# Three edits to the issue order of a fused four-layer kernel: the first two weighings of a block made adjacent, the start of the second block rearranged, and the value copies of the second block moved ahead of its exponentials

## The reference, cut to what matters

```
x = x + pooled_attention(x)          # tanh scorer, masked softmax over 32 tokens, weighted sum of tokens
x = x + multi_head_attention(x)      # 16 heads of 8, softmax(Q K^T * scale + bias) V, then Wo
x = x + low_rank_expert_ffn(x)       # relu(x Wi + common + expert[row]) Wo + common + expert[row]
x = x + gelu_ffn(x)                  # gelu(x fc1 + b), 96 shared columns + 32 columns of expert[row]
```

## Time and profile before

| | us |
|---|---|
| median of 3 runs | 261.66 (261.25 to 266.24) |
| the profiled execution, whole time | 262.47 |
| its span from first to last instruction | 260.7 |
| PE busy | 248.1 (95% of the span) |
| DVE busy | 186.5 (72%) |
| ACT busy | 137.7 (53%) |
| POOL busy | 120.2 (46%) |

### The profile page before, as it was taken

How to read it: one execution, slowest core, us unless ns; L and a number is a source line. 1 busy time by engine, 2 the same in 40 slices (tenths; PEclk the granted TensorE clock), 3 DMA queues, 4 the chain that set the end, 5 groups by cost and what they waited for, 6 DMA issues and landing times.

```text
span 260.7 us, 12683 instructions
## 1 busy us (share of the span) xinstructions
PE 248.1 (95%) x4866; PEld 184.0 (71%) x4866; DVE 186.5 (72%) x349; ACT 137.7 (53%) x253; POOL 120.2 (46%) x242
## 2 busy tenths in 40 slices
PE   7899999888999999999999999999999999988994
PEld 5575556666687867787777768686878587857983
DVE  4879877874878877888878787878787878562031
ACT  3075563374628745673748382757196437542250
POOL 5867513454516452554445443536154436455330
PEclk9999999999999999999999999999999999999999
DMA  6979304640355216530554045603554541165011
GB/s 184 381 236 266 83 3 162 237 173 5 100 212 204 100 24 238 204 140 0 211 208 184 0 164 204 236 0 121 201 203 177 215 174 43 57 230 205 3 43 43
DMA packets 27326, 38.27 MB, mean 147 GB/s; under 512 B 10769, under 2 KB 11537, under 8 KB 27170
## 3 DMA queue, kind: packets, MB, share of 16 engines
q1 hardware_dynamic: 26578, 36.99, 39.7%
q10 hardware_dynamic: 720, 0.89, 1.3%
HBM read 10.60 MB, written 2.10 MB: 49 GB/s over the span
## 4 chain that ended last, share of the span: by engine, by line
PE 84%; DVE 8%; ACT 3%; issue 2%; DMA 2%; POOL 0%; ACTq 0%; DVEq 0%; POOLq 0%
PE pB L783 12%; PE pB L866 9%; PE pB L736 7%; PE pB L740 6%; PE pooled L711 6%; PE pB L737 6%; PE pooled L679 5%; PE pV L726 4%; PE pV L691 3%; PE pooled L673 3%; PE pV L732 2%; PE pooled L640 2%; PE pB L818 2%; DMA cols_s<-cols_dram 2%; PE pB L843 1%
## 5 line engine op out<-in xcount | busy, mean ns | idle before, releaser
L403 POOL COPY rw<-e3t_s 128x128 f32 x128 | 38.6, 302 | 55.1 <-issue 51.2
L382 POOL TENSOR_TENSOR sc<-sc,rmax 128x512 f32<-128x512 f32 x32 | 33.6, 1051 | 49.8 <-DVE rmax L1164 49.8
L783 PE MATMUL pB<-rwo,hid 128*32 128x128 f32 x1024 | 33.6, 275 | 1.2 <-issue 1.2
L507 ACT ACTIVATE ex<-sc 128x512 f32<-128x512 f32 x32 | 20.2, 630 | 27.2 <-POOL sc L382 26.7
L783 PEld LDWEIGHTS pB<-rwo,hid 128*32 128x32 f32 x1024 | 26.6, 109 | 5.1 <-issue 4.0
L1159 DVE SCALAR_TENSOR_TENSOR sc<-pooled,bias 128x512 f32<-128x512 f32 x32 | 21.7, 678 | 11.3 <-PE pooled L711 9.7
L413 POOL COPY rwo<-weff 128x512 f32 x32 | 21.9, 688 | 14.2 <-issue 5.6
L1170 DVE STREAM_TRANSPOSE pt<-ex 128x512 f32<-128x512 f32 x32 | 22.4, 701 | 7.2 <-ACT ex L507 7.1
L511 ACT ACTIVATE hid<-pB 128x512 f32<-128x512 f32 x32 | 18.3, 595 | 14.8 <-PE pB L740 14.6
L866 PE MATMUL pB<-rw,hT 128*32 128x128 f32 x768 | 24.4, 274 | 0.0
L1164 DVE TENSOR_REDUCE rmax<-sc 128x16 f32<-128x512 f32 x32 | 22.0, 686 | 1.1
(11 more groups left out here) (181 smaller groups left out, 521.7 us busy)
## 6 DMA issues: line engine op xcount, KB each, us to landing
rwo<-weff SPq DMA_DIRECT2D x96, 256.0 KB, 2.3
rw<-fc2t_dram SPq DMA_DIRECT2D x4, 768.0 KB, 12.3
xT<-xt_dram SPq DMA_DIRECT2D x7, 256.0 KB, 2.6
xN<-xn_dram SPq DMA_DIRECT2D x7, 256.0 KB, 2.9
out_dram<-o_s SPq DMA_DIRECT2D x7, 256.0 KB, 2.3
e3t_s<-e3t_dram SPq DMA_DIRECT2D x1, 1024.0 KB, 10.6
rwo<-ffn_w_dram SPq DMA_DIRECT2D x1, 896.0 KB, 6.3
rwo<-ffn_w_dram SPq DMA_DIRECT2D x1, 512.0 KB, 11.3
```

The lines of the kernel that those rows point to most:

```text
L382: pool.tensor_tensor(sc[:, g % 2, :, :], sc[:, g % 2, :, :], rmax[:, g % 2, :].unsqueeze(2).to_broadcast([P, H, S]), ALU.subtract).then_in ...
L403: pool.tensor_copy(rw[:, r, :, SHARED:D], e3t_s[:, bass.ds(e, 1), :, :].rearrange("p o c n -> p (o c) n"))\
L783: last = mm(pB2[S * q:S * q + S, P * g:P * g + P], hid[:, c, tok], rwo[:, Q4 * g + q, c, :], start=(c == 0), stop=(c == FC - 1))
```

## The change

It has three parts, and all of them are changes of order.

- In every `step_of(n)` for n from 1 to 7, PE issues `weigh(n, 0)` behind chunk 2 of the hidden layer in place of ahead of it, so that it stands directly in front of `weigh(n, 1)`.
- In front of step 1, PE issues `attn_out(0)` and `pooling(1)` ahead of `pairs_out(1)`, and `keep_busy(4, ...)` there is dropped. The waits are fitted to that: `pooling(1)` waits for `weff_sb` 2, `low(0)` for `weff_sb` 5, and the wait for all eight copies stands behind `low(0)`. ACT does `x2_high(0)` first and the four copies of the second half behind it, in the order 2, 0, 1, 3, and each of them waits for all products of `pairs_out(1)` (`weff_ps` 8).
- In step 1 alone, ACT does `values(1)` ahead of `l0_exps(2)` and `exps(1, 0)`, in place of behind them.

```
@@ ACT @@
             def expert_out(half, j):
-                act.wait_ge(weff_ps, Q4 * half + j + 1)
+                act.wait_ge(weff_ps, 2 * Q4 if half == 1 else j + 1)
...
             weight_highs(N_I, W_I, F)
+            x2_high(0)
+            expert_out(1, 2)
             expert_out(1, 0)
             expert_out(1, 1)
-            expert_out(1, 2)
             expert_out(1, 3)
-            x2_high(0)
...
                     token_major(last)
+                if last is None:
+                    values(n)
                 if next_block:
                     l0_exps(n + 1)
                 exps(n, 0)
-                values(n)
+                if last is not None:
+                    values(n)
                 exps(n, 1)
@@ PE @@
             base_out(1, 3)
+            attn_out(0)
+            pe.wait_ge(weff_sb, 2)
+            pooling(1)
             pairs_out(1)
-            pe.wait_ge(w_high, 2)
-            attn_out(0)
-            pe.wait_ge(weff_sb, 5)
-            pooling(1)
-            pe.wait_ge(weff_sb, 6)
-            keep_busy(4, pS0, ffn_p[0])
...
                 if last is None:
-                    pe.wait_ge(weff_sb, 2 * Q4)
+                    pe.wait_ge(weff_sb, Q4 + 1)
+                    pe.wait_ge(w_high, 2)
                     pe.wait_ge(w_low, 1)
                     low(n - 1)
+                    pe.wait_ge(weff_sb, 2 * Q4)
...
                 hidden_expert(n - 1, 1)
-                weigh(n, 0)
                 hidden(n - 1, 2)
                 hidden_expert(n - 1, 2)
+                weigh(n, 0)
                 weigh(n, 1)
```

## The result

| | before | changed |
|---|---|---|
| median of 5 runs, us | 261.66 | 258.51 |
| profiled execution, us | 262.47 | 258.46 |
| its span, us | 260.7 | 256.7 |

The ratio of the changed kernel's time to the time before is 0.9894, with a 95% interval of 0.9874 to 0.9914: 1.1% faster, within the 2% named in the prediction. Some executions took about 4 us longer, two of the five before among them (266.2 and 266.3; without them its median is 261.42): the ratios leave such runs out, and two later profiles that fell on one, at a granted clock of 0.98, are not read. The forecast was 258.6. The number was met; the way to it, as the rest of this text shows, was different in each of the three parts.

A forecast was written before the change was run, and what follows sets the result against it. PE, busy for 95% of the span, was taken as the bound. 0.93 + 1.0 + 1.4 = 3.3 us gave 259.1 from the profiled execution or 258.3 from the median; 258.6 was taken, range 257.2 to 260.8.

The forecast's parts named there:

- The front: Start of step 1: without the four idle-filling products the queries start at 39.46 against 40.39, gaining 0.93 us if nothing is late.
- the 0.21 put on the filler alone: Start of step 1: deleting only the idle-filling products, without the swap, would gain 0.21 us, as queries wait for `x1T`.
- The values: Step 1: block 1's value copies move into ACT's idle time, removing PE's whole 1.0 us wait; bounds 0.6 to 1.0.
- The pair: First two weighings in a row: one turn of 0.2 us less in each of 7 steps, 1.4; bounds 0 to 2.5.
- The gathers: Last `out_rows` group of step 1: PE arrives at 58.57, last gather lands about 58.6; a tie counted as 0.
- rival 1: Gathers hold PE up in step 1: first gather slips 2.0 us, PE waits 1.4, time 260.0; chance 0.14.
- first sign of being wrong: In the changed profile, PE waiting for the gathers of the last group would show the prediction wrong.
- The stall of 1.18: PE's "issue" gap in step 1's last output group, likeliest instruction fetch, left as it is; bounds 0 and 2.1 us.
- rival 3: The instruction-fetch stall in step 1 goes or is covered, saving 1.2 us more: 257.4; chance 0.07.
- The base: The 3.3 us sum gives 259.1 from the profiled 262.47, or 258.3 from the runs' median 261.66; 258.6 taken.
- Rivals 2: The pair of weighings brings nothing while the other two parts hold: 260.0; chance 0.13.
- rival 4: Loop body no longer stays resident: five passes each pay a 1.18 us fetch stall, 5.9 in all, 264.5; chance 0.04.

## Why the prediction was right, and where it wasn't

The time came out as forecast, 258.51 for 258.6, and the sign and size stand. The parts do not: that the sum held is luck, errors of nearly the same size on either side.

1. **The front, 0.93.** The queries' and DVE's times came as worked out (keys on DVE at 41.36, forecast 41.41; 0.95 at `values(1)`). The step that failed is "if nothing is late next": the copies into `weff` end 2 later, POOL's copies with them, and they lie on DVE's `lowp_l`, 0.98 for 0.69. That makes 0.65 at the scores. The time gave 0.65 alone, and nothing measurable beside the pair. That `x1T` needs the pairs as cover was right (0.78 of wait without them); the 0.21 put on the filler alone was 0.
2. **The values, 1.0.** Right alone (1.06). Wrong in the sum: the prediction priced each part against the kernel before. The pair moves the first weighing by 1.4, behind the end of the copies, and by itself covers the same wait. Beside it the edit is worth at most the 0.54 that PE would wait for the transposition, and the times don't show even that. The prediction had both numbers, the copies' end at 52.98 and chunk 2 ahead of the weighing, and didn't set them side by side.
3. **The pair, 1.4.** Undersized. Per step 0.2 of turn was right (one product at 0.43 fewer), and two weighings take 0.70 in place of 0.80, which makes 0.3. What the sum lacked is the last step, 0.96 where 0.2 was counted, since POOL's and DVE's instructions no longer meet there, and step 1, 0.71 where 0.2 was counted, with the covered wait in it. Measured alone: 3.1 us by the medians and the profiles, above the upper bound of 2.5, though the interval of the ratio (2.1 to 3.8) takes that in. Weight loads run beside products, with PEld busy for 183.9 and PE for 245.5 of a span of 256.7, and yet the turn isn't free. Within the pair the loads run through, 64 in 0.66 with one idle stretch of 0.35 ahead of them, where the kernel before has such a stretch of 0.35 ahead of 32 loads in 0.35.
4. **The gathers, 0.** The wait of rival 1 happened, though not its time of 260.0, and with it what the prediction had named as its first sign of being wrong: PE waits 1.3 and 1.4 in two profiles, for a forecast tie at 58.6. PE came as forecast (58.70 for 58.57), and the first issue slipped as computed (0.46 for 0.5 to 0.6). What failed is the landing. The last gather of before had landed at 58.30 and not "by 58.0", its issue slipped by 0.71, and it took 3.6 and 3.8 in place of 2.64, at 59.97 and 59.82 instead of 58.6.
5. **The stall of 1.18, left as it was.** It went where the wait for the gathers stands. The counting of records shows that its place is fixed in PE's list, and nine profiles show 0.3 to 1.2 of it. That the prediction kept it and set the gathers' wait at nothing was wrong twice, by nearly the same amount (1.2 and 1.3): this, and the double count of the values and the full 0.93 of the front against the undersized pair, is why the sum held. Of rival 3 the first half happened, the stall was covered, and its gain went into the gathers.
6. **The base.** Against the median, 261.66 - 3.3 = 258.3 was nearer than 259.1, from the profiled execution's 262.47, which held a long stall.

Rivals 2 (the pair is worth nothing) and 4 (stalls in every pass of the loop) are refuted: the pair alone gives 1.1%, and no profile has an "issue" gap of that kind in the loop. What the trace has on a loop body that stays resident, the condition of rival 4, are packets: the instruction queue q8 has none between 93.1 and 213.8 in the kernel before, and none between 91.1 and 209.1 in the changed one. Each stretch holds the last four passes of the loop whole, so nothing that rival 4 feared began with the change.

## What to carry to other kernels

Price edits against each other and not only against the kernel before: of two edits that attack one wait, the second is worth what is left of it, and a consumer that moves back may cover a wait for nothing. Look for alternations of small matmul groups with large ones in PE's list; each turn cost 0.2 to 0.3 here, it repeats every step, and moving the small groups together costs nothing while the engine behind them has room, which its start times show. When PE gets faster, follow the transfers and the engines that work on a fixed pace, here gathers with one issue in 1.2, the gap of 0.3 to 1.2 at a fixed count in PE's own list and POOL's copies, most of them 0.74 apart, since they are what it runs into. When a forecast sum comes out right, measure its parts before you trust it.

## What the runs showed of the hardware that I hadn't expected

- A VectorE subtraction of 128x512 of two SBUF tensors takes 0.68 alone and up to 1.33 (1.38 to 1.40 in three later runs) while GpSimd works on a tensor_tensor of 128x512, and another 0.69 alone and 0.98 beside GpSimd's copies.
- A gap in PE's list without a releaser stands at a fixed count of instructions (behind 6 records of the group, behind 10 when 8 are missing ahead). It lasted 1.18 and 0.45 in two profiles of one and the same program, 0.3 to 1.2 over nine profiles, and ends 1.2 to 1.45 behind the end of a 16 KB packet on an instruction queue.
- Of twelve equal gathers the landing times ranged from 2.3 to 4.5 in one profile of the kernel before, and the last of them took 3.6 and 3.8 in the two profiles of the changed kernel. Over eight profiles, gathers beside a packet of the instruction queue q8 took 3.2 in the median, those beside no instruction packet 2.3.
